# A decoder layer on one core: the scaling of a quad's attention outputs is written apart from their transpose, and two of the scalings are moved to other steps

## What is computed

```python
# q: x (8, 512, 256); k, v: ctx (8, 1024, 256); 16 heads of 16 columns
qh = (q @ Wq.T).reshape(B, QL, 16, 16)
kh = (k @ Wk.T).reshape(B, KL, 16, 16)
vh = (v @ Wv.T).reshape(B, KL, 16, 16)
attn = jnp.einsum('bnhc,bmhc->bhnm', qh, kh) * 16 ** -0.5
attn = jax.nn.softmax(attn, axis=-1)
out = jnp.einsum('bhnm,bmhc->bnhc', attn, vh).reshape(B, QL, 256)
x = _layernorm(x + out @ Wo.T + bo)
```

## Time and profile before

| | us |
|---|---|
| median of 3 runs | 1798.39 (1798.37 to 1799.76) |
| the profiled execution, its own time | 1802.73 |
| span of the profiled execution, first to last instruction | 1801.0 |
| PE busy (share of the span) | 1659.4 (92%) |
| DVE busy | 1262.2 (70%) |
| ACT busy | 816.1 (45%) |
| POOL busy | 594.7 (33%) |

### The profile page before, as it was taken

How to read it: one execution, slowest core, us unless ns; L and a number is a source line. 1 busy time by engine, 2 the same in 40 slices (tenths; PEclk the granted TensorE clock), 3 DMA queues, 4 the chain that set the end, 5 groups by cost and what they waited for, 6 DMA issues and landing times. The chain is left out here.

```text
span 1801.0 us, 48927 instructions
## 1 busy us (share of the span) xinstructions
PE 1659.4 (92%) x19922; PEld 800.2 (44%) x19922; DVE 1262.2 (70%) x2377; ACT 816.1 (45%) x983; POOL 594.7 (33%) x969
## 2 busy tenths in 40 slices
PE   6899999999999799999999999999999999888564
PEld 3566666666666423343343433433433333234332
DVE  5767677667675587878878889788788798721005
ACT  2334344344343225656656556566556565551003
POOL 3635545555543446125043061160430510000002
PEclk8999999999999769999999999999999999899777
DMA  7000000000000130211212202112112022366994
GB/s 257 3 4 3 3 3 3 3 3 3 3 32 15 37 103 22 66 57 44 82 35 73 83 27 75 57 43 67 48 61 96 15 87 88 137 256 247 421 417 166
DMA packets 66254, 146.10 MB, mean 81 GB/s; under 512 B 12384, under 2 KB 36320, under 8 KB 58368
## 3 DMA queue, kind: packets, MB, share of 16 engines
q1 hardware_dynamic: 65488, 142.41, 21.8%
q10 hardware_dynamic: 560, 0.72, 0.2%
HBM read 92.43 MB, written 7.86 MB: 56 GB/s over the span
## 5 line engine op out<-in xcount | busy, mean ns | idle before, releaser
L1718 DVE TENSOR_REDUCE mx<-cpsV 128x1 f32<-128x512 f32 x1024 | 652.4, 684 | 120.4 <-PE cpsV L1428 98.3
L1625 ACT ACTIVATE w<-cpsA 128x1024 f32<-128x1024 f32 x512 | 496.3, 1021 | 255.9 <-PE cpsA L1489 250.8
L1428 PE MATMUL cpsV<-w 96*128 96x512 bf16 x1024 | 333.6, 395 | 27.5 <-DVE mx L1718 17.1
L1489 PE MATMUL cpsA<-w 99*128 99x512 bf16 x1024 | 273.0, 381 | 5.8 <-ACT w L1603 3.4
L1450 PE MATMUL cacc<-w 128*32 128x512 f32 x2048 | 274.3, 608 | 0.4 <-ACT w L1625 0.4
L469 PE MATMUL psA<-w 128*128 128x512 f32 x512 | 257.6, 627 | 8.3 <-DVE WT L1106 3.5
L1428 PEld LDWEIGHTS cpsV<-w 96*128 96x128 bf16 x1024 | 85.4, 98 | 307.8 <-DVE mx L1718 228.9
L1683 POOL TENSOR_TENSOR crstd<-cmv,eps 128x4 f32<-128x4 f32 x8 | 1.6, 201 | 589.0 <-DVE cmv L1791 589.0
L766 ACT COPY w<-psA 128x1024 f32<-128x1024 f32 x64 | 64.8, 1012 | 231.8 <-PE psA L469 231.8
L1489 PEld LDWEIGHTS cpsA<-w 99*128 99x128 bf16 x1024 | 93.8, 98 | 136.1 <-ACT w L1625 10.9
L886 POOL TENSOR_TENSOR VP<-V,VPF 128x128 f32<-128x128 f32 (+2 forms) x256 | 129.2, 535 | 42.6 <-PE psA L482 36.8
(11 more groups left out here) (226 smaller groups left out, 2194.3 us busy)
## 6 DMA issues: line engine op xcount, KB each, us to landing
w<-in_w SPq DMA_DIRECT2D x56, 1024.0 KB, 16.0
w<-w SPq DMA_DIRECT2D x189, 128.0 KB, 2.3
w<-w SPq DMA_DIRECT2D x189, 64.0 KB, 2.0
w<-in_ctxT SPq DMA_DIRECT2D x8, 1024.0 KB, 5.1
w<-in_xT SPq DMA_DIRECT2D x8, 512.0 KB, 7.1
x_tok<-in_x SPq DMA_DIRECT2D x8, 512.0 KB, 9.5
w<-in_w SPq DMA_DIRECT2D x8, 512.0 KB, 17.5
out_y<-w SPq DMA_DIRECT2D x16, 256.0 KB, 2.3
```

Of the source, the lines that this page charges most:

```text
L1428: nc.tensor.matmul(out, Qst[q // 2][0:ROWS, hh, g * P:(g + 1) * P], Kst[q // 2][0:ROWS, hh, half * BANK:(half + 1) * BANK], start=True, st ...
L1489: last = nc.tensor.matmul(out[:, n * T:(n + 1) * T], Kst[q // 2][0:ROWS + 3, hh, chunk * P:(chunk + 1) * P], Qst[q // 2][0:ROWS + 3, hh, : ...
L1625: nc.scalar.activation(Pr[:, (2 * s + pp) % 4, :], src, ACT.Exp, scale=CA_SCALE).then_inc(act_evac, 1)
L1718: nc.vector.tensor_reduce(mx[:, q % 2, row, k % 2:k % 2 + 1], full(m[k]), AX_X, ALU.max).then_inc(dve_evac, 1)
```

## The change

`outputs` is cut into two functions. `scale_outputs` has the reciprocal, the multiplication and their drains; `turn_outputs` has the wait for `o_moved`, the transpose and its drain. The calls are:

- quad 0: scaled in step 9 (`SCALE_OUTPUTS`), between the first two and the last two reductions of the step; transposed in step 12, where both were before;
- quad 1: both in step 20, as before;
- quad 2: scaled in step 0 of the next batch, after the step's first two reductions and ahead of `take_outputs` of quad 3; transposed in step 1, where both were. In the last batch both stay in step 27;
- quad 3: both in step 1 of the next batch, as before.

```diff
-                def outputs(bb, q):
+                def scale_outputs(bb, q):
...
+                def turn_outputs(bb, q):
+
+                    t = byq[q % 2]
                     dve.wait_ge(o_moved[q % 2], bb * 32 + (q // 2 + 1) * 16)
...
                     if prev and s == 1:
                         if sec != "tail":
-                            outputs(b - 1, 2)
-                        outputs(b - 1, 3)
+                            turn_outputs(b - 1, 2)
+                        scale_outputs(b - 1, 3)
+                        turn_outputs(b - 1, 3)
...
                             if now:
-                                outputs(b, 0)
+                                turn_outputs(b, 0)
                             nc.vector.max(m8[:], L[:])
...
+                    if now and s == SCALE_OUTPUTS:
+                        scale_outputs(b, 0)
...
+                    if prev and s == 0 and sec != "tail":
+                        scale_outputs(b - 1, 2)
                     if now and s and s % KT == 0:
                         take_outputs(b, s // KT - 1)
```

More of the change, by code:

```diff
@@ L137 @@
 PROJECT_K, X2T, COPY_X2, GATE, GATE_MAX, GATE_EXP, TOP8, TOP8_T, PICK, PICK_T = (7, 12), 9, 10, 10, 12, 14, 20, 21, 28, 29
-PROJECT_V0, LAST_OUTPUTS = 20, 27
+PROJECT_V0, LAST_OUTPUTS, SCALE_OUTPUTS = 20, 27, 9
 BEHIND_JOBS = (PROJECT_V1 + 1, PROJECT_K[0] + 1)
@@ L1835, in body @@
                                                   ).then_inc(dve_evac, 1)
+                    if now and s == SCALE_OUTPUTS:
+                        scale_outputs(b, 0)
                     if sec == "first" and s == GATE_MAX:
-                        outputs(b, 0)
+                        turn_outputs(b, 0)
                     if now and s == TOP8:
-                        outputs(b, 1)
+                        scale_outputs(b, 1)
+                        turn_outputs(b, 1)
                     if sec == "last" and s == LAST_OUTPUTS:
-                        outputs(b, 2)
+                        scale_outputs(b, 2)
+                        turn_outputs(b, 2)
+                    if prev and s == 0 and sec != "tail":
+                        scale_outputs(b - 1, 2)
                     if now and s and s % KT == 0:
```

## The result

| | us |
|---|---|
| before, median of 17 runs | 1798.39 (1795.06 to 1800.32) |
| changed, median of 17 runs | 1802.17 (1797.65 to 1808.08) |
| ratio changed to before | 1.0026, interval 1.0018 to 1.0033 |
| changed, the profiled execution's own time and its span | 1802.06; 1800.3 |

The change makes the kernel slower by 3.8 us, a little more than a measurement can tell from no change. The forecast was 0.7 us slower. The runs of the changed kernel also spread over 10 us, those of before over 5.

A forecast was written before the change was run, and what follows sets the result against it. PE was taken as the bound. Gains of 4.5 + 0.9 = 5.4 us against costs of 5.5 + 0.6 = 6.1 us made it 0.7 us slower: 1799.1 us from the median 1798.39, range 1795.5 to 1802.0.

The forecast's parts named there:

- PE is the bound: Mid batch of 121.5 us: PE has 118.7 us of matmuls, DVE 102.6; moved scaling counts only by PE's waits.
- Step 12: Quad 0's scaling leaves here; DVE stops holding PE, gaining 0.75 us in each of six mid batches, 4.5 us in sum.
- Step 12 of the last batch: Scaling stands after the DMA of `L`, uncovered; its removal gains 0.9 us and PE's idle falls from 3.71 to 2.8.
- Step 9: Quad 0's scaling goes into DVE's 0.93 us idle: cost zero in seven batches, 0.6 us in batch 0.
- Step 1: Quad 2's scaling leaves here; DVE already idles 0.52 us, which only grows to 1.4: gain zero in seven batches.
- Step 0: Quad 2's scaling delays a reduction PE waits for: 0.91 us in each of batches 2 to 7, 5.5 us in sum.
- The clock at the batch starts: PE's wait grows from 0.60 to about 1.5 us; clock may fall in one or two batches, 1.5 us each.
- Its own sign of being wrong: Prediction is wrong if a mid batch changes by over 0.5 us or the clock after the last batch's idle stays up.
- Rival B: Last batch's shorter PE idle, 2.8 us, keeps the clock up: 5.0 us faster, 1794.1 us; chance 0.12.
- C: Step 12 gives nothing, as DVE's 0.53 us idle ends by an event at its own time: 1803.6 us; chance 0.06.
- D: Scaling in step 0 is hidden, PE's matmul being late for something other than DVE: 1793.6 us; chance 0.04.

The follow-up runs named there:

- the filled wait: Changed kernel, with PE doing the matmul ahead of its long wait at batch starts six times instead of once: 1800.31 us, ratio 1.0011 to the kernel before.

## Why the prediction was wrong

- **PE is the bound, and a block on DVE counts only by the waits that it causes.** Right. The differences between the mid batches that were followed up here are in such waits or in the clock behind one.
- **Step 12 gives 0.75 us in each mid batch.** Right: 1.72 us became 0.97. Batch 1, which has no cost at its start, is shorter by 0.72.
- **Step 12 of the last batch gives 0.9.** The idle fell by 1.00 us, of which 0.17 is a shorter wait for the DMA of `L` in that execution.
- **Step 9 costs nothing, 0.6 in batch 0.** Right: no wait in the mid batches, 0.60 in batch 0. One term in it was mis-sized, with no effect on the time: the multiplication takes 0.80 us there and not 0.43 (below), so from its start (939.00) to the next reduction (940.27) it is 1.27 us in place of 0.91, and it uses some of the lateness that PE tolerates.
- **Step 1 gives nothing.** Right: DVE's idle there only grows, from 0.52 to 1.42 us in batch 3 of the changed kernel, where the clock stays up.
- **Step 0 costs 0.91 us.** Right for the wait: 0.60 became 1.53 us, 0.93 more, in batches 2 to 6, and 0.79 us in batch 7. With the scaling behind the last two reductions the wait is 0.60 us again, so it is the place ahead of that reduction that costs.
- **The clock at the batch starts.** This is the step that failed. The prediction named it, but called it a smaller thing, took "one or two of the batches" at 1.5 us, and put it in the range and not in the sum. Its own sign of being wrong came true: a mid batch changed by 1.8 us, more than 0.5. What the traces show in its place are 8 falls in three executions, 2.7 on average, seven at about 1.6 us and one at 3.0: 4.7 us in an execution, more than the net of all else. With it the sum is 0.7 + 4.7 = 5.4 us. Against that stands the last batch, whose low stretch was 10.2 and 6.8 us long in the two traces of before and 3.4, 6.8 and 6.8 us in those of the changed kernel. Half of the difference of the means, about 1.4 us, comes back. 4.0 us are left, and 3.8 were measured. The close match is partly luck, since five traces give the means, and the filled wait gave back only 2.7 us.
- **Rival B, the clock of the last batch.** It did not stay up, neither at 2.71 nor at 1.86 us of idle; the row at 1667.91 was the right guide. But what this row says of 2.8 us it says of 1.5 us as well. I used it to set B aside and did not carry it, in the sum, to the waits that the change itself brings to 1.5 us. It is a weaker guide to those than it looks, since PE was not dense ahead of it:

```profile
1664.00:1668.00 4.00, 2.28 (x32) 1.47 (x28) 0.42 (x1) 1.43 (x2) 0.24 (x1) 1.00 1.02 424
```

  By the Trainium skill ("TensorE: Matmul & The Clock Gate", section "Why this matters for your kernels") none of these gaps would be long enough; the traces show otherwise, with falls at gaps of 1.53, 1.86 and 2.71 us.
- **Rivals C and D.** Neither came. In step 12 of the changed kernel the reduction behind the logits starts 0.86 us ahead of PE's second scores (952.57 and 953.43), where it started 0.06 us behind them (952.11 and 952.05), so DVE is 0.92 us earlier. C's suspicion of the 0.53 us had some truth: written out, that idle is gone. Whether it moved with the work in the loop is not shown, since the 0.53 us of idle that DVE has there now ends with a matmul of PE.
- **The range.** Its upper end, 1802.0, allowed for one or two falls, and the time is 1802.17.

## What to carry to other kernels

Price a longer wait of TensorE by its length and by its clock: look for the shortest idle in the trace at which the clock fell, see how dense PE was ahead of it, and count every place that the change brings near it. Where a small block moves between steps, its place within the step decides: behind the reduction for which PE waits it was free, ahead of it cost 0.9 us and the clock. And where an engine is late at the same place in every round, see first whether its own loop makes it so; writing out DVE's batches gave 9 us, more than any move of a block.

## What was not expected of the hardware

- The clock fell at idle times of 1.53 and 1.86 us of an otherwise nearly dense stream of matmuls, and not each time: at the same wait of 1.53 us it fell at 8 of 15 places. Seven of these falls lasted 3.4 us and one 6.8. A number of falls that differs between executions fits the wider spread of the changed kernel's runs; that the spread comes from it is not shown.
- The multiplication of the scaling takes twice as long where GpSimd works. DVE in step 9 of batch 2 of the changed kernel:

```profile
939.32 0.80 DVE L1754 TENSOR_TENSOR byq<-byq,rec 128x256 f32<-128x256 f32 x1
940.27 0.69 DVE L1718 TENSOR_REDUCE mx<-cpsV 128x1 f32<-128x512 f32 x1 [0.15 <-PE cpsV L1428]
```

  And POOL at the same time:

```profile
939.23 2.50 POOL L190 TENSOR_TENSOR w<-w,zero 128x256 bf16<-128x256 f32 x4
```

  In step 0, with POOL idle, it takes 0.43 us. Those with POOL at work beside them all the time took 0.80 to 0.82 us in this kernel, all without it 0.43. The price is not fixed: in the written-out form of the changed kernel the seven in step 9 with POOL at work took 0.43 to 0.91 us. The Trainium skill ("GPSIMD Engine Reference", section "1. Specifications") names contention of GpSimd with VectorE instructions that have two inputs in SBUF, as this one has; the trace agrees.
- The hardware loop costs DVE 1.96 us at its branch (1.90 to 2.25 us at others) and idle of half a microsecond in step 12, and both are gone when it is written out. What makes them was not tried apart.
